# Graph network on one core: everything between the second and the third edge pass put into one phase pipelined by tiles

## The reference, cut to what matters

```python
    # L1: out = attention-weighted sum over the edges and one self loop a node
    h = gat_conv(layer_norm(x, ln1_g, ln1_b), ...) + gat_b     # 4 heads of 32
    h = h + x_in                                 # x_in: relu(layernorm(x))
    hn = layer_norm(h, ln2_g, ln2_b)
    ffn = gelu(hn @ w1 + b1) @ w2 + b2           # 128 -> 256 -> 128
    x = x + (h + ffn)
    # L2: the table of the third edge pass
    feat = relu(layernorm(x))
    rows = feat * clip(out_deg, 1.0) ** -0.5     # gathered by the edges
```

## Time and profile before

| | |
|---|---|
| median of 3 runs | 9781.4 us (9772.96 to 9783.71) |
| the profiled execution's own time | 9776.25 us |
| its span in the trace | 9774.5 us |
| first DVE operation of `l1post` | 4963.97 us from the span's start |
| SP's first load of `edges2` | 5225.12 us |

### The profile page before, as it was taken

How to read it: one execution, slowest core, us unless ns; L and a number is a source line. 1 busy time by engine, 2 the same in 40 slices (tenths; PEclk the granted TensorE clock), 3 DMA queues, 4 the chain that set the end, 5 groups by cost and what they waited for, 6 DMA issues and landing times. The chain is left out here.

```text
span 9774.5 us, 168717 instructions
## 1 busy us (share of the span) xinstructions
PE 6805.1 (70%) x43003; PEld 5615.8 (57%) x43004; DVE 4654.5 (48%) x12164; ACT 2957.9 (30%) x7513; POOL 6425.7 (66%) x6673
## 2 busy tenths in 40 slices
PE   4978888888727777777743444444447888888875
PEld 3767777777616666666632333333335667666664
DVE  4156666666566666666663222222234444444443
ACT  1345555555314444444420000000012222222222
POOL 0167777777527777777724777777746777777760
PEclk9977777777755555555565555555567766677777
DMA  3333333333212222222212222222213333333320
GB/s 109 150 108 104 104 104 104 104 104 104 76 30 54 54 54 54 54 54 54 54 28 47 53 53 53 53 53 53 53 35 99 101 101 100 100 101 102 101 72 15
DMA packets 378679, 733.92 MB, mean 75 GB/s; under 512 B 168442, under 2 KB 219185, under 8 KB 371926
## 3 DMA queue, kind: packets, MB, share of 16 engines
q0 software_dynamic: 251264, 621.88, 24.3%
q1 hardware_dynamic: 99818, 100.52, 3.3%
q10 hardware_dynamic: 27500, 10.39, 0.4%
HBM read 655.46 MB, written 76.88 MB: 75 GB/s over the span
## 5 line engine op out<-in xcount | busy, mean ns | idle before, releaser
L461 POOL DMA_INDIRECT edges_rows<-gat_rows,edges_idx_r x1568 | 1580.6, 1008 | 539.5 <-issue 425.2
L461 POOL DMA_INDIRECT edges_rows<-kv_rows,edges_idx_r x1568 | 1584.6, 1011 | 501.6 <-issue 480.4
L461 POOL DMA_INDIRECT edges_rows<-kv_typed,edges_idx_r x1568 | 1536.3, 980 | 530.4 <-issue 474.4
L461 POOL DMA_INDIRECT edges_rows<-conv_rows,edges_idx_r x1568 | 1499.0, 956 | 568.3 <-issue 466.7
L985 PE MATMUL edges_ps_sum<-edges_rows,edges_pick 128*128 x3520 | 875.7, 430 | 1192.1 <-POOLq L465 1135.9
L609 PE MATMUL edges_ps_sum<-edges_wv,edges_pick 128*128 128x132 f32 x7040 | 1609.1, 398 | 3.4 <-ACT edges_pick L659 1.6
L985 PEld LDWEIGHTS edges_ps_sum<-edges_rows,edges_pick 128*128 128x128 f32 x3520 | 764.7, 322 | 1303.0 <-issue 1303.0
L609 PEld LDWEIGHTS edges_ps_sum<-edges_wv,edges_pick 128*128 128x128 f32 x7040 | 1370.6, 287 | 150.3 <-issue 121.6
L1083 PE MATMUL edges_ps_q<-q,edges_pick_t 128*128 x3520 | 724.7, 371 | 351.3 <-DVE edges_prod L1138 347.1
L1083 PEld LDWEIGHTS edges_ps_q<-q,edges_pick_t 128*128 128x128 f32 x3520 | 634.4, 270 | 432.2 <-issue 429.7
L1005 DVE TENSOR_TENSOR sums<-sums,edges_ps_sum 128x129 f32 x440 | 127.5, 290 | 1576.7 <-PE edges_ps_sum L985 1576.7
(11 more groups left out here) (340 smaller groups left out, 11411.1 us busy)
## 6 DMA issues: line engine op xcount, KB each, us to landing
kv_typed<-l0pre_out SPq DMA_DIRECT2D x49, 1024.0 KB
edges_rows<-kv_typed,edges_idx_r POOLq DMA_INDIRECT x1568
edges_rows<-gat_rows,edges_idx_r POOLq DMA_INDIRECT x1568
edges_rows<-conv_rows,edges_idx_r POOLq DMA_INDIRECT x1568
edges_rows<-kv_rows,edges_idx_r POOLq DMA_INDIRECT x1568
edges_feat_r<-visit_features ACTq DMA_DIRECT2D x660, 10.0 KB
x<-in_x SPq DMA_DIRECT2D x2, 3136.0 KB
kv_rows<-l3pre_kv SPq DMA_DIRECT2D x49, 128.0 KB
```

The lines of the kernel that those rows point to most:

```text
L461: pool.indirect_dma_start(rows[:, k, g * width:(g + 1) * width], None, table, bass.IndirectOffsetOnAxis(ap=idx_r[:, k, g:g + 1], axis=0)). ...
```

## The change

The phases become one, `conv_inputs`. Work runs in steps `i` of a software pipeline: `in_turn(49, (late, work), ...)` calls each piece of work for tile `i - late`, so every engine's stream is unrolled and the pieces of one tile lie in different steps. DVE and POOL also work by sets of 7 tiles (`CH = 7`, `SETS = 7`). Layer norms use BN_STATS and BN_AGGR in place of the passes over the whole buffer; ACT applies them as scale and bias of an activation, with gamma and beta in the copy from PSUM; the out degree is folded into the second norm's scale. POOL weights the self loops, adds the biases and clears `sums`. The table is stored by sets.

```diff
-        gat_output(nc, c, w, h[:], sums[:, 0:NT * 132], q[:], top[:], own[:], dram)
-        for_rows(nc, "ln2g", w["L1_gnn_ln2_g"], w["L1_gnn_ln2_b"], q[:], h[:], square, add=x[:])
-        feed_forward(nc, "ffn1", c, w["L1_gnn_w1"], w["L1_gnn_b1"], w["L1_gnn_w2"], w["L1_gnn_b2"], ACT.Gelu, h[:], x[:])
-        norm_phase(nc, "ln2", x[:], h[:], square, relu=True)
+        conv_inputs(nc, c, w, x[:], h[:], sums[:], q[:], top[:], own[:], out_deg[:], dram)
         conv = sums[:, 0:NT * (D + 1)]
-        conv3 = conv.rearrange("p (t f) -> p t f", t=NT)
-        conv_table(nc, h[:], out_deg[:], conv3, dram)
-        clear_sums()
         conv_pass(nc, "edges2", c, dram, res, dram["conv"], dram["idx_src"], conv)
...
+class TileNorm:
+    def count(self, nc, rows, t):
+        nc.vector.bn_stats(self.stats[:, t, :], rows).then_inc(self.counted, 1)
+    def close(self, nc, dve, t):                 # every 7th tile
+        dve.wait_ge(self.counted, t + 1)
+        for u in range(t + 1 - CH, t + 1):
+            ins = nc.vector.bn_aggr(self.mv[:, u, :], self.stats[:, u, :])
+        ins.then_inc(self.joined, 1)
+        dve.wait_ge(self.joined, k + 1)
+        nc.vector.tensor_scalar(self.rstd[:, few], self.mv[:, few, 1], LN_EPS, None, ALU.add).then_inc(self.raised, 1)
+    def root(self, nc, act, t):                  # every 7th tile
+        act.wait_ge(self.raised, k + 1)
+        nc.scalar.activation(self.rstd[:, few], self.rstd[:, few], ACT.Sqrt).then_inc(self.rooted, 1)
+    def settle(self, nc, dve, t, factor=None):   # every 7th tile: reciprocal, times factor, shift
...
+def conv_inputs(nc, c, w, x, h, sums, g, top, own, out_deg, dram):
+        lag, late = 12, 32
...
+            @block.gpsimd
+            def _(pool):
+                pool.wait_ge(loaded, 112)
+                pool.wait_ge(weighed, 1)
+                for k in range(SETS):
+                    pool.wait_ge(selves_in[k], 16)
+                    nc.gpsimd.tensor_tensor(own_rows, own_rows, bcast(shares[:, 1, few(k), :], [P, CH, 4, 32]), ALU.mult).then_inc(selves_weighed, 1)
+                    nc.gpsimd.tensor_tensor(rest, rest, bias, ALU.add).then_inc(selves_joined, 1)
+                    pool.wait_ge(selves_weighed, k + 1)
+                    pool.wait_ge(selves_joined, k + 1)
+                    nc.gpsimd.tensor_tensor(heads_of(rest), heads_of(rest), own_rows, ALU.add).then_inc(selves_done, 1)
+                    nc.gpsimd.tensor_tensor(x[:, few(k), :], x[:, few(k), :], rows[:, 1, :].unsqueeze(1).broadcast_to([P, CH, D]), ALU.add).then_inc(biased, 1)
+                for k in range(SETS):
+                    pool.wait_ge(g_made, k + 1)
+                    nc.gpsimd.memset(sums[:, k * CH * 132:(k + 1) * CH * 132], 0.0).then_inc(cleared, 1)
...
+            @block.tensor
+                in_turn(NT, (lag, turn_rows), (lag + 2, hide), (lag + 4, show))
...
+            @block.scalar
+                def normalise(t):
+                    act.wait_ge(first.ready, t // CH + 1)
+                    if t >= 2:
+                        act.wait_ge(flat_done, t - 1)
...
+                in_turn(NT, (3, lambda t: first.root(nc, act, t)), (24, lambda t: second.root(nc, act, t)), (late, make_row),
+                        (lag, normalise), (lag + 1, copy_flat), (lag + 3, gelu))
...
+            @block.vector
+                def join_selves(t):                  # every 7th tile
+                    nc.vector.tensor_tensor(heads, heads, bcast(shares[:, 0, few(k), :], [P, CH, 4, 32]), ALU.mult).then_inc(heads_done, 1)
+                    dve.wait_ge(heads_done, k + 1)
+                    dve.wait_ge(selves_done, k + 1)
+                    nc.vector.tensor_tensor(heads_of(g[:, few(k), :]), heads, heads_of(h[:, few(k), :]), ALU.add).then_inc(g_made, 1)
...
+                in_turn(NT, (4, lambda t: first.settle(nc, dve, t)), (25, lambda t: second.settle(nc, dve, t, out_deg)),
+                        (0, join_selves), (lag + 5, add_out), (1, count_first), (lag + 6, count_second),
+                        (2, lambda t: first.close(nc, dve, t)), (lag + 7, lambda t: second.close(nc, dve, t)), (14, start_x))
```

More of the change, by code:

```diff
@@ L1530, in _ @@
                 link(nc.vector.memset(acc, 0.0))
[L1533 to L1570, removed]
@@ L1642, in _ @@
                 node_tiles(dve, body)
[L1646 to L1654, removed]
-            @block.vector
-            def _(dve):
-                link = Chain(dve, steps)
-                nc.vector.tensor_scalar(out_deg, out_deg, 1.0, None, ALU.max).then_inc(clipped, 1)
-                dve.wait_ge(rooted, 1)
-                link(nc.vector.reciprocal(out_deg, out_deg))
-                nc.vector.memset(part[:, :, D:D + 1], 1.0)
-                nc.vector.tensor_tensor(part[:, :, 0:D], h, bcast(out_deg, [P, NT, D]), ALU.mult).then_inc(ready, 1)
-            @block.sync
-            def _(sp):
-                sp.wait_ge(ready, 1)
-                sp.dma_start(dram["conv"].rearrange("(t p) f -> p t f", p=P), part).then_inc(stored, 16)
-                sp.wait_ge(stored, 16)
 def conv_output(nc, c, w, x, acc, g):
@@ L1977, in graph_layers @@
                      a_dst[:], hist=out_deg[:], spare=q2[:, 0:WIDE * GE].bitcast(BF16))
-        gat_output(nc, c, w, h[:], sums[:, 0:NT * 132], q[:], top[:], own[:], dram)
-        for_rows(nc, "ln2g", w["L1_gnn_ln2_g"], w["L1_gnn_ln2_b"], q[:], h[:], square, add=x[:])
-        feed_forward(nc, "ffn1", c, w["L1_gnn_w1"], w["L1_gnn_b1"], w["L1_gnn_w2"], w["L1_gnn_b2"], ACT.Gelu, h[:], x[:])
-        norm_phase(nc, "ln2", x[:], h[:], square, relu=True)
+        conv_inputs(nc, c, w, x[:], h[:], sums[:], q[:], top[:], own[:], out_deg[:], dram)
         conv = sums[:, 0:NT * (D + 1)]
-        conv3 = conv.rearrange("p (t f) -> p t f", t=NT)
-        conv_table(nc, h[:], out_deg[:], conv3, dram)
-        clear_sums()
         conv_pass(nc, "edges2", c, dram, res, dram["conv"], dram["idx_src"], conv)
-        conv_output(nc, c, w, x[:], conv3, q[:])
+        conv_output(nc, c, w, x[:], conv.rearrange("p (t f) -> p t f", t=NT), q[:])
         norm_phase(nc, "ln3", x[:], h[:], square, relu=True)
```

161 lines of the change are left out of this document (added).

## The result

The changed kernel takes 9681.76 us (median of 4 runs, 9678.99 to 9687.31) against 9781.21 (4 runs, 9772.96 to 9783.71) for the kernel before on the same chip: ratio 0.990, with a 95% interval of 0.9883 to 0.9918. That is 99 us less. The forecast was 9665 (116 us less), the range 9636 to 9692.

A forecast was written before the change was run, and what follows sets the result against it. Engines take turns in the 261.15 us section before the edge pass, all of it replaced; start 30, steps 104, tail 4.5, store 5.7 and barrier 0.7 make 145 us, 116 less: 9665 us, range 9636 to 9692.

The forecast's parts named there:

- start, to the first normalised tile: New phase's start: loads 8.5 us, then POOL's and DVE's work on two sets, written out in turn, 21.5 us; 30 us.
- steps 12 to 63: Pipeline steps up to the last Gelu: 36 at 2.0 us, 16 at 1.75, 4 us for lower clock; 104 us.
- tail: After the last Gelu: second product, addition, last norm's statistics, root and settle, seven rows of the table; 4.5 us.
- store and barrier: End of the phase: store of the last set 5.7 us, barrier before the next edge pass 0.7 us.
- the phase is lost one for one: Section before the edge pass: what it loses of its 261.15 us, the whole kernel loses; 116 us.
- That is 1.14 us: ACT's work per step: two Gelus 0.63 us, three copies or scalings starting 0.17 us apart.
- 8.9 + 2.0 + 1.5: Time per set in the steps: PE's pace, loss at table loads, root's wait for DVE; 12.3 us, 1.75 a step.
- rival 2: PE falls to 1.2 GHz between bursts: a step is 2.54 us, 28 us more, 9693 us; chance 0.1.
- Rival 1: Pipeline fits tighter, POOL and DVE hardly collide, table loads hide: steps 1.5 us, start 26, 9634 us; chance 0.2.
- Rival 3: A switch of tables drains ACT at each of 17 loads: near 9685 us; chance 0.05.
- Rival 4: Change is slower: engine streams in lockstep, each step one tile's round trip, 4.0 us at 1.2 GHz; chance 0.02.
- Rival 5: Gain does not arrive, since the next edge pass waits for something else, a transfer from before the barrier; chance 0.02.

The follow-up runs named there:

- the plain copy: Changed kernel with gamma and beta folded into w1 and Gelu's bias, so the copy from PSUM has no operand: phase 160.0 us, 9672.41 us.
- the full product: Changed kernel with b2 added by a TensorE product of all 128 rows in place of POOL's additions: phase 162.0 us, 9676.35 us.

## Why the prediction was right, and where it was off

The forecast's sum and the trace, term by term:

| term | forecast | measured | from |
|---|---|---|---|
| start, to the first normalised tile | 30 | 30.4 | 4964.05 to 4994.44 |
| steps 12 to 63, to the last Gelu's end | 104 | 115.6 | to 5110.03 |
| tail, to the last row | 4.5 | 9.8 | to 5119.81 |
| store and barrier | 6.4 | 5.3 | to 5125.14 |
| phase | 145 | 161.1 | |

**That the phase is lost one for one** held: 100.0 us off the phase, 99 off the median.

**The start** was right in its sum, and its parts about so: POOL's first work waited until SP's loads had landed, and an operation of 896 numbers took 1.9 to 2.4 us on average where 1.85 was reckoned. The second join ended 26.8 us in, where the sum had 26.2.

**The steps: the mechanism was right, the term of ACT mis-sized.** What was wrong is "That is 1.14 us", three copies at 0.17 and two Gelus at 0.63. The rows at 0.17 were of plain copies; here all three have pointers, and the step is 1.62 us. Times 49 that is 24 us more of ACT. The Trainium skill, "ScalarE: Activation LUTs", section "What ACT_TABLE_LOAD costs", has the rule that was not applied: each pointer operand adds about 93 ns to an ACTIVATE, and operations back to back overlap by as much. By that an estimate is 293, 386 and 479 ns for none, one and two pointers; the runs have 275, 366 to 403 and 460 to 496, and 91 to 94 ns less for a scale left out, so the trace agrees. The runs price it: leaving the scale out took 13.6 us from ACT and 5.3 from the phase. That only part comes through, and 0.8 where 9 us were saved by the plain copy, shows that ACT is not the bound in every step. The step that follows, that PE sets the pace between table loads, at 1.27 us, fell too (half of the second product less: 1.0 us).

In the second half ACT is busy over 95%. With the price put right the sum of ACT is 7 x 1.62 + 3.0 = 14.3 us a set; the three sets of tiles from 21 to 42 took 14.9, 15.3 and 14.9 us, where 12.3 was reckoned. So a step is 2.15 us there in place of 1.75. The first three sets took 16.4, 18.1 and 17.3 us, 2.5 a step, where 14 and 2.0 were reckoned; the first 25 steps are 60.0 us. DVE is busy for 47.28 us of the 59.6 from 4994.4 to 5054.0, so it is not the bound by its sum alone. Most time is lost at the step at which DVE joins a set. The normalises, elsewhere in these sets some 1.2 us apart, stand 8.0 us apart there:

```profile
5014.98 0.53 ACT L1992 ACTIVATE l2pre_normed<-q,l2pre_ln2g_shift,l2pre_ln2g_rstd 128x128 f32<-128x128 f32 x1
...
5023.01 0.48 ACT L1992 ACTIVATE l2pre_normed<-q,l2pre_ln2g_shift,l2pre_ln2g_rstd 128x128 f32<-128x128 f32 x1
```

DVE works without a pause from 5013.55 to 5022.85, 9.3 us where the sum had 5.4 (and 0.8 for each operation beside POOL), and the four roots behind the start wait 3.2 us on average where 1.5 was reckoned; then ACT has its table loads, and DVE waits. It was DVE and POOL, as said, but with DVE's joins at 2.35 us on average over the phase (2.85 while POOL works) and even the smallest DVE operation waiting, 1.24 us for an addition of seven numbers, until POOL's operation ends:

```profile
5001.79 2.91 POOL L1944 TENSOR_TENSOR h<-h,l2pre_rows 128x896 f32<-128x896 f32 x1
...
5003.49 1.24 DVE L1854 TENSOR_SCALAR l2pre_ln2g_rstd<-l2pre_ln2g_mv 128x7 f32<-128x7 f32 x1
```

Halving POOL's work (12.0 us, 6.7 of it before the first tile), moving all of it to DVE (2.9 us longer) and moving the roots (3.1 us) bear on it from three sides; how the first half's excess divides among them is open. The steps missed by 11.6 us though ACT had 24 us more to do, since part of that fell into time in which ACT had been waiting.

**The tail** was reckoned with seven rows. `make_row` is at `late` = 32 steps, Gelu at `lag` + 3 = 15, so 17 tiles' rows come after the last Gelu in ACT's stream. The first starts at 5109.92, just before that Gelu's end; the timeline above has the other 16, 6.3 us at 0.39, and one more table load and 1.51 us for a table buffer that the store still had. This was in the order of the instructions, and was missed.

**BN_STATS** started 0.20 us apart with a duration of 0.28, and seven BN_AGGR lasted 0.56: the values taken, 0.2 and 0.1, were near.

**The signs.** Met were the first tile at 30 us, the waits of ACT at the roots, DVE stretched beside POOL and table loads without a gap. Not met: the clock of 1.00 (0.61 to 0.81), and DVE busy over 70%, which it was in the first two windows (25.41 and 22.27 of 30) but not in the last two (17.28 and 11.96). A step of over 2.4 us was to show the prediction wrong: the mean is 2.2, but the sets from tile 7 to 21 had 2.6 and 2.5. Two sums are off by little: 8.9 + 2.0 + 1.5 is 12.4, and rival 2's 0.55 us a step is counted from 2.0, where the forecast's own mean was 1.9; from that it would be some 31 us and not 28.

**The rivals.** Rival 1 did not come: POOL and DVE collided, and the start was 30 us. Rival 2 had half of it: the granted clock was 0.61 to 0.81 in the steps, not 1.00, but PE at that clock was little waited for (ACT at Gelu 3.2 us); it began to count when ACT got shorter. Rival 3, the drain at a switch of tables: loads of 1283 ns with 0.1 us of idle time in all before each group of eight, and 0.9 us each on the phase. The operation behind one starts as the load ends:

```profile
5100.13 0.44 ACT L1999 ACTIVATE l2pre_flat<-l2pre_ps_flat,l2pre_cols 128x128 f32<-128x128 f32 x1
...
5100.59 1.28 ACT L2006 ACT_TABLE_LOAD   x1
...
5101.88 0.63 ACT L2006 ACTIVATE l2pre_hidden<-l2pre_ps_hid,l2pre_b 128x128 f32<-128x128 f32 x2
```

What is lost besides is the overlap of the two operations around it, some 0.1 us. By the Trainium skill, "ScalarE: Activation LUTs", "What ACT_TABLE_LOAD costs", a switch costs 2.66 us in all; an estimate by it is 40 us for 15 of them, and the run without them gave back 13.4. The trace does not agree with a drain here. Of rival 4, the lockstep, there is a trace: one wait taken away came back for the most part as another, but at 2.2 us a step on average, far from the 4.3 that it needed. Rival 5 did not come, as the first term shows.

## What to carry to other kernels

When phases that took turns are merged into one pipeline, add up each engine's work with rows of the same form, operands included: the price of an activation with two pointers is not that of a copy. Then ask of the order how many items of the last stage are still to do when the first stage ends; that is the tail. And before moving an addition onto TensorE because it has time to spare, give the product all its rows, and price it: here even the full product gained nothing.
